# One core, a chain of four convolution blocks: the last group's D and F stages in parts of one, one and two images, its tiles 12 plan units apart, and the first tiles of a group placed 24 units later

## What is computed

```
x = x + focal_modulation(gn(x))    # stages A, B, C
x = x + fp8_gated_mlp(gn(x))       # stage L
x = x + spectral_scan(gn(x))       # stage D (and the start of F)
x = x + deform_conv(gn(x))         # stage F, and the tiles
```

```
offsets = conv3x3(x, offset_w) + offset_b
val = sum over 4 corners of gather(corner) * weight
out = einsum('bhwkc,kcf->bhwf', val, kernel) + bias
```

## Time and profile before

| | |
|---|---|
| median of 3 runs | 5486.43 us (5479.14 to 5493.68) |
| the profiled execution | 5502.65 us, span 5500.9 us |
| PE, DVE, ACT, POOL busy | 55%, 60%, 31%, 52% |
| mean granted clock of TensorE | 0.67 |

### The profile page before, as it was taken

How to read it: one execution, slowest core, us unless ns; L and a number is a source line. 1 busy time by engine, 2 the same in 40 slices (tenths; PEclk the granted TensorE clock), 3 DMA queues, 4 the chain that set the end, 5 groups by cost and what they waited for, 6 DMA issues and landing times. The chain is left out here.

```text
span 5500.9 us, 92960 instructions
## 1 busy us (share of the span) xinstructions
PE 3035.7 (55%) x39574; PEld 2637.7 (48%) x39574; DVE 3300.6 (60%) x4063; ACT 1728.7 (31%) x3209; POOL 2874.9 (52%) x2614
## 2 busy tenths in 40 slices
PE   2973235559744466569744466579744463454333
PEld 2872135459633365459633365469633353443222
DVE  4347843575678755565688656574788655454333
ACT  1223424621234235421233235421234242232000
POOL 1000000475566765565566655674666666677776
PEclk9965555569667766659767666659766666655555
DMA  6841184569633585559633576559633564754333
GB/s 164 171 91 22 33 133 138 141 147 224 146 96 102 129 193 169 148 135 222 146 94 105 133 178 173 153 144 236 139 107 98 144 172 136 173 171 131 112 106 93
DMA packets 776703, 763.09 MB, mean 139 GB/s; under 512 B 575185, under 2 KB 652401, under 8 KB 771857
## 3 DMA queue, kind: packets, MB, share of 16 engines
q1 hardware_dynamic: 651873, 417.24, 34.2%
q0 software_dynamic: 124416, 339.90, 21.8%
HBM read 637.12 MB, written 136.73 MB: 141 GB/s over the span
## 5 line engine op out<-in xcount | busy, mean ns | idle before, releaser
L2124 POOL DMA_INDIRECT e_gb<-corner_table,e_idx x2592 | 2860.3, 1104 | 2606.5 <-DMA e_cws<-cw_all 1097.6
L2186 DVE TENSOR_TENSOR e_vw<-e_gb,e_pc 128x1024 f32<-128x1024 f32 x576 | 774.9, 1373 | 710.4 <-DMA e_gb<-corner_table,e_idx 681.0
L2152 PE MATMUL e_pv<-shifts,e_vw 128*128 128x128 f32 x2744 | 536.7, 364 | 480.7 <-DVE e_vw L2193 480.7
L2152 PEld LDWEIGHTS e_pv<-shifts,e_vw 128*128 128x128 f32 x2744 | 440.0, 190 | 513.5 <-DVE e_vw L2193 491.2
L488 PE MATMUL e_pw<-wk,e_vt 128*64 128x64 f32 (+1 forms) x2880 | 324.4, 285 | 351.6 <-DVE e_xr L2204 220.3
L488 PEld LDWEIGHTS e_pw<-wk,e_vt 128*64 128x64 f32 (+1 forms) x2880 | 279.2, 192 | 413.7 <-issue 246.5
L2162 ACT ACTIVATE e_vt<-e_pv 128x512 f32<-128x512 f32 x288 | 183.6, 638 | 731.2 <-PE e_pw L2152 730.4
L502 PE MATMUL b_p<-b_x,b_tt 100*100 100x96 f32 x4096 | 396.2, 258 | 25.7 <-DMA b_tt<-zl_copies 25.0
L502 PEld LDWEIGHTS b_p<-b_x,b_tt 100*100 100x100 f32 x4096 | 388.6, 176 | 29.1 <-DMA b_tt<-zl_copies 28.2
L1921 ACT ACTIVATE f_xall<-f_p 64x384 f32<-64x384 f32 (+2 forms) x320 | 301.7, 1056 | 130.7 <-PE f_p L1816 128.4
L2193 DVE TENSOR_TENSOR e_vw<-e_vw 128x1152 f32<-128x1152 f32 x233 | 331.6, 1423 | 8.0
(11 more groups left out here) (309 smaller groups left out, 7147.3 us busy)
## 6 DMA issues: line engine op xcount, KB each, us to landing
b_tt<-zl_copies SPq DMA_DIRECT2D x256, 234.0 KB, 9.7
b_tt<-zl_copies SPq DMA_DIRECT2D x128, 390.0 KB
e_gb<-corner_table,e_idx POOLq DMA_INDIRECT x2592
d_px<-x_halo SPq DMA_DIRECT2D x32, 1152.0 KB
corner_table<-f_xn SPq DMA_DIRECT2D x128, 288.0 KB
f_xall<-xpad SPq DMA_DIRECT2D x10, 2400.0 KB, 16.7
x_halo<-d_xo SPq DMA_DIRECT2D x128, 144.0 KB
d_wd<-wd_rows SPq DMA_DIRECT2D x8, 1890.0 KB, 30.8
```

Of the source, the lines that this page charges most:

```text
L2124: nc.gpsimd.indirect_dma_start(self.gb[k][:, 4 * q:4 * q + 4, :].rearrange("p a c -> p (a c)"), None, T.table[m], off)\
L2152: last = nc.tensor.matmul(dst, vw[:, a, 2 * q:2 * q + nq, :].rearrange("p k c -> p (k c)"), T.ident[:, :], start=(a == 0), stop=(a == n - ...
L2186: v.tensor_tensor(dst, self.gb[k][:, 4 * k0:4 * k1, :].rearrange("p (k a) c -> p k a c", a=4), bc(w, [128, k1 - k0, 4, C], 3), ALU.mult).t ...
```

## The change

Group 3 gets three parts, of one, one and two images. `steps` of StageF and some conditions learn a part of one image; since parts can now be odd, the semaphore counts of the two alternating input buffers are taken from a new field `seen` rather than from `base // 2`. The space between group 3's tiles becomes 12.0 plan units in place of 9.0. Where the next placed image sets `due`, it sets `clock + 24.0`.

```diff
         if k == 1:
             self.st.enter(sp, P.G, P.stage)
-            load_x(1)
+            if P.n > 1:
+                load_x(1)
...
-        if k < 2 and p == 0:
+        if k < min(2, P.n) and p == 0:
             gn.pe_sum(pe, self.psn, NH, gn.of(P, 0, k))
         if 0 <= m < P.n:
             if p == 0:
-                pe.wait_ge(self.p_in[m % 2], 48 * (P.base // 2 + m // 2 + 1))
+                pe.wait_ge(self.p_in[m % 2], 48 * (P.seen[m % 2] + m // 2 + 1))
...
     def steps(n):
 
+        if n == 1:
+            return [10, 14, 6] + [12, 16, 6] + [12, 10, 8] + [1]
         return [10, 14, 6] + [16, 22, 6] + [22, 26, 6] * (n - 2) + [16, 20, 6] + [12, 10, 8] + [1]
...
-            load(0)
-            load(1)
+            for m in range(min(2, P.n)):
+                load(m)
...
             if mid:
+                if not new and not old:
+                    between()
                 moves(0)
                 moves(1)
...
-Part = namedtuple("Part", "G first n base turn stage")
+Part = namedtuple("Part", "G first n base turn stage seen")
...
-    parts, turn = [], 0
+    parts, turn, seen = [], 0, (0, 0)
...
-            parts_of_group.append(Part(G, first, n, G * NI + first, turn, 4 + 2 * len(parts_of_group)))
-            first, turn = first + n, turn + 1
+            parts_of_group.append(Part(G, first, n, G * NI + first, turn, 4 + 2 * len(parts_of_group), seen))
+            first, turn, seen = first + n, turn + 1, (seen[0] + (n + 1) // 2, seen[1] + n // 2)
...
-PARTS = parts_of([(NI,)] * (NGRP - 1) + [(2, 2)])
+PARTS = parts_of([(NI,)] * (NGRP - 1) + [(1, 1, 2)])
...
-    spaces = [(b - a) / (NI * J) for a, b in zip(starts, starts[1:])] + [9.0]
+    spaces = [(b - a) / (NI * J) for a, b in zip(starts, starts[1:])] + [12.0]
...
                 if tiles == J * loaded:
-                    due = clock
+                    due = clock + 24.0
```

More of the change, by code:

```diff
@@ L1550, in square @@
         def square():
-            act.wait_ge(self.x_in[k % 2], 64 * (P.base // 2 + k // 2 + 1))
+            act.wait_ge(self.x_in[k % 2], 64 * (P.seen[k % 2] + k // 2 + 1))
             if m >= 1:
@@ L1613, in sums @@
         def sums():
-            dve.wait_ge(self.x_in[k % 2], 64 * (P.base // 2 + k // 2 + 1))
+            dve.wait_ge(self.x_in[k % 2], 64 * (P.seen[k % 2] + k // 2 + 1))
             gn.dve_sums(dve, NH, xs[:, 3:NR + 3, :], self.sq, gn.of(P, 0, k))
@@ L1999, in dve @@
         if p == 1 and j < P.n:
-            dve.wait_ge(self.x_in[j % 2], 16 * (P.base // 2 + j // 2 + 1))
+            dve.wait_ge(self.x_in[j % 2], 16 * (P.seen[j % 2] + j // 2 + 1))
             for g in range(3):
```

## The result

| | before | after |
|---|---|---|
| median, 14 runs each | 5486.89 us (5479.14 to 5499.29) | 5469.26 us (5462.32 to 5485.58) |
| ratio of after to before, 95% interval | | 0.9967 (0.9957 to 0.9977) |
| the profiled execution | 5502.65 us | 5480.97 us |

The account below looks back on a forecast made before the run. The end was taken as the stages' placing of an image plus POOL's gathers for the tiles left: 4453.6 + 230 + 295 + 453.2 = 5431.8 us, 69 less than the 5500.9 span. Off the median: 5417 us, range 5372 to 5475.

Parts of the forecast that it names:

- I take 25 us a group ... 75: DVE's wait at a group's first tile goes: 25 us in each of three groups, image 12 placed 75 us (36 to 99) earlier.
- Tile 72 would start its weighing some 35 us after the placing: Group 1 on DVE: image 7's addition and sums come first, so tile 72 starts some 35 us after image 4's placing.
- the wait is filled: At the groups' first tiles another engine takes over, saving 12 us a group: 39 us less gain, 5456 us; chance 0.16.
- The closer tiles of group 2 cost nothing here: Group 2's tiles at 14.8 units for 15.6: no cost ahead of image 12, and POOL still keeps up.
- One tile a group moves ... nothing in the sum: One tile a group leaves stage F for the next stage: about 4 us of DVE work moves, nothing in the sum.
- The first part has one image fewer ... 51 us: Group 3's first part, stages D and F: 41.1 us less D and 10 us less F, 51 us (41 to 63) earlier.
- I take 230 for image 12 to 13: Group 3, between these placings: 230 us, between 220.5 from the stages and 236.9 from POOL's 12 tiles.
- I take 295 for image 13 to 14: Group 3, between these placings: 295 us, with 276.6 from the stages and 308.7 at the most from 17 tiles.
- The last 36 tiles: From image 14's placing to the end: 12 us, 36 x 11.74 = 422.8 of POOL's gathers and 18.4, together 453.2 us.
- The check from POOL's side: Over the last 72 tiles, 845 us of gathers in 978: 102 us lost for 45.7 before, for a start 126 us earlier.
- The heads are shorter: Heads of group 3's parts wait for tiles, not data: 83 us in place of 96, time 5363 us; chance 0.11.
- The extra part costs more than it brings: Image 13 to 14 repeats the old 386.5 us: 91.5 us more, 5508 us, slower than before; chance 0.08.

## Why the prediction was wrong

The direction held, the size did not. Against its own sum of spans (5431.8) the profiled span of 5479.3 is 47.5 us longer. It comes from two terms, since 28.2 (image 12) - 6.9 (12 to 13) + 27.7 (13 to 14) - 1.5 (the rest) = 47.5.

**"I take 25 us a group ... 75" was too much; it measured about 39.** Image 12 was placed at 4481.8 for 4453.6, 28.2 us late: 36 too little from this term, 8 more than I had taken from the next (4579.6 - 4481.8 = 97.8, of which 58.7 are the next term's). The cycles did shorten by 15.6, 21.7 and 23.8 us in groups 0, 1 and 2 (67.0 to 51.4, 72.8 to 51.1, 74.5 to 50.7), 61.1 in sum, not 75. The step that failed is "Tile 72 would start its weighing some 35 us after the placing": I read the row of tiles off the order up to the first `e_vw` and took image 7's work as 35 us; it was there after 22.0, and I did not look at what stood behind it. Tile 72's first half began 23.6 us after the placing, where 22.8 stood before: image 7's work filled the wait, it did not push the tile behind its gather. And tile 73 stood behind it in the same step, so DVE was paced by POOL for a second tile. Of 29.0 us of waiting 14.0 were left. Larger delays confirm it: with 40 units 5.9 us of waiting are left in group 1 and the cycle is 43.1 us, with 56 units none and 40.2 us. The rival "the wait is filled" came near the size at image 12 (12 a group, 39 less gain) by chance, not by its mechanism: no other engine took over, DVE itself was still held.

The rest of the 61.1, some 21 us, was given back downstream. Image 4 was to come 25 us earlier and came 0.9 later, image 8 came 39 earlier for 50. From the last of those cycles to the end of the next group's stage L it took 12 us more in sum (2446.0 for 2434.1): 3.4 more in group 0, 14.8 less in group 1, 23.4 more in group 2 (837.9 for 814.5). Another 5 went between the end of L and the placings, 4 ahead of the first cycle. This is where **"The closer tiles of group 2 cost nothing here"** and **"One tile a group moves ... nothing in the sum"** fell. The tiles that the delay holds back have to be weighed in the stages behind, and DVE is the engine in which those stages wait. With group 2's old spacing that stretch took 824.8, with the delay alone 824.2, and with the closer tiles but no delay 830.7. I put some 13 us on the closer tiles and some 10 on the displaced ones. Equal orders differ by up to 18 us between two runs in such a stretch (in group 1 815.1 and 801.7, before and without the delay; in group 0 794.0 to 811.6 in the seven kernels with 24 units). So the differences of groups 0 and 1 are not told from chance. Group 2's is larger than that spread: the four kernels with 24 units and the closer tiles took 837.9 to 848.5 there. Its division is an estimate. Nor were the 215 tiles ahead of image 12 right; there were 214.

**"The first part has one image fewer ... 51 us" held.** From the end of L to image 12's placing 183.3 us passed for 242.0, 58.7 fewer; between the kernel with the delay alone and the one after, image 12 came 55.4 us earlier.

**"I take 230 for image 12 to 13" held:** 223.1, with 48.0 us from patches to first product where I took 50.

**"I take 295 for image 13 to 14" was too little:** 322.7. The head took 98.4 for 96, but D from its first product to its end took 99.8 for 80.0, and F from there to the placing 124.5 for 95.6. The prediction had two bounds for this stretch, 276.6 from the stages and 308.7 from the tiles ("17 tiles, 12.5 each"), took less than the larger, and the measured time lies above both. What failed is to treat them as rivals, of which one or the other holds. SP and DVE behind the head, after:

```profile
4773.66 31.57 SPq L1448 DMA_DIRECT2D x_halo<-d_xo  x14
...
4810.00 1.21 SPq L1456 DMA_DIRECT2D d_px<-x_halo  x3
```

```profile
4803.29 0.61 DVE L1638 TENSOR_TENSOR region<-d_p,region 96x192 f32<-96x192 f32 x2
...
4834.02 1.49 DVE L2191 TENSOR_TENSOR e_vw<-e_gb,e_pc 128x1280 f32<-128x1280 f32 x1 [22.38 <-DMA e_gb<-corner_table,e_idx]
...
4862.87 0.35 DVE L1638 TENSOR_TENSOR region<-d_p,region 96x192 f32<-96x192 f32 x1 [19.10 <-ACT region L1561]
```

The wait of 22.38 us is nothing new: the stretch of the earlier trace rows has the same one. The waits of DVE there, from 4742 to 5017 before, and from 4803 to 5027 after, for gathers and for stage D:

```profile
DVE e_vw L2186 <- DMA e_gb<-corner_table,e_idx: 109.9, 25, 21.8
DVE region L1637 <- ACT region L1560: 2.9, 1, 2.9
```

```profile
DVE e_vw L2191 <- DMA e_gb<-corner_table,e_idx: 58.9, 11, 22.4
DVE region L1638 <- ACT region L1561: 19.1, 1, 19.1
DVE region L1672 <- ACT region L1600: 10.8, 1, 10.8
```

Before, DVE waited there for gathers and hardly for D, so 12.5 us a tile was the pace of the gathers. After, it waited for both in turn, and the 17 tiles took 13.2 us each. The second image's first product came 59.6 us after the first image's, where I had taken the 41.1 of the earlier trace rows. Why it came so late is open: its patches were issued at 4810.0, 6.7 us behind the first product (0.1 us ahead of it in the second part of before), but with the delay alone this distance was 37.0 us, with its patches issued ahead of the first product by 22.4.

**"The last 36 tiles" held:** 451.7 for 453.2.

**The check from POOL's side** gave the warning and I did not use it as one. It said that POOL would lose 102 us for 45.7; it lost 119. What I left out is the comparison that the experiments then made: the same delay without the parts starts POOL later and loses only 39 (884.5 - 845). The prediction put both parts of the change in one sum and never asked whether one of them alone would be better.

**The rivals.** "The heads are shorter" said that a head waits for its tiles and not its data, against the DMA share of 0.94 to 0.98. The heads took what I forecast, so its time did not come; but the copies lengthened them by 2.8 and 9.3 us and did not move the placing, so its doubt about the DMA share was in part sound. The 436 GB/s that the Trainium skill gives on the page "DMA: Bandwidth & Descriptors", section "Anatomy of one DMA — SWDGE (gpsimd) path", were not reached here either: 241 GB/s is the most over a head in these runs. "The extra part costs more than it brings" was right in sign, and wrong in its size as I priced it (from image 12 to 14 the kernel after took 545.8 us, the point of decision was 594): it costs 20 us by the medians (33 by the ratios) against the delay alone, not 91 against the forecast.

## What to carry to other kernels

- Where an engine runs in order and mixes two kinds of work, count how many waiting items stand in a row, not only the first: a delay that clears the first tile's wait and leaves the second tile behind it brings only part of the gain (cycle 51.1 us, 43.1 with the second moved too).
- An earlier start of a producer is worth only what it does not lose on the way. Put the start and the loss in one number (end = start + work + starving), for each part of a change by itself.
- A stretch's pace per tile holds for the wait that set it. Where the engine also waits for stages, the two bounds can add up: forecast at most 308.7 us, measured 322.7.

## What was not expected of the hardware

With the 16 DMA engines 0.96 to 0.99 busy in heads of 48 to 58 us, copies of 3.78 MB behind its loads raised the rate over the head from 204 to 231 GB/s and from 217 to 241, and did not delay the work behind: in these heads the busy share did not tell how much more the engines could carry. And the same 14 DMAs of `store` took 11.24 us to issue with little but gathers beside them and 31.57 us while patches, weights and gathers were under way. The run with the copies bears on the cause: with them under way as well, the same 14 issues took 44.47 us (at 4773.30), while the first image's store, ahead of the loads, took 10.98. So the more was under way, the longer SP took to issue.
